# The row factor of a graph attention reaches all partitions through HBM instead of through TensorE

## The reference

```
h = maximum(layernorm(x), 0)
x = x + graph_attention(h, adj, W0, a0)     # layer 0
x = x + multi_relation(h, adj, a0..a3)      # layer 1: scores between nodes, softmax
x = x + relational_conv(h, adj, W, bias)    # layer 2
x = x + elu(graph_attention(h, adj, W3, a3))# layer 3

graph_attention: Wh = h @ W; s1 = Wh @ a1; s2 = Wh @ a2
  e = leaky_relu(s1[i] + s2[j], 0.2); where adj <= 0: -9e15
  out = softmax(e) @ Wh
```

## Time and profile before

| | |
|---|---|
| median of 3 runs | 299.83 us (299.61 to 300.18) |
| profiled execution | 299.55 us, of it the span 297.7 us |
| PE busy | 279.9 us, 94% of the span |
| weight loads of PE (PEld) | 259.4 us, 87% |
| DVE busy | 261.3 us, 88% |
| ACT busy | 260.2 us, 87% |
| POOL busy | 224.8 us, 76% |
| chain that ended last | PE 67%, DVE 20%, ACT 6% |

### The profile page before, as it was taken

The page is one execution under the profiler, slowest core; times in us unless marked ns, Lnnn a source line. Parts: engine busy times, 40 slices in busy tenths (PEclk is TensorE's granted clock), DMA queues, the critical chain, the costliest instruction groups (busy, mean ns, idle before and its releaser), DMA issues.

```text
span 297.7 us, 8186 instructions
## 1 busy us (share of the span) xinstructions
PE 279.9 (94%) x2250; PEld 259.4 (87%) x2250; DVE 261.3 (88%) x1355; ACT 260.2 (87%) x849; POOL 224.8 (76%) x363
## 2 busy tenths in 40 slices
PE   1899999999998999999999999999999899999992
PEld 1799998888987999998888999998888799999991
DVE  2689999888888898999999999988888889799995
ACT  3799997799999985899999889799999998589993
POOL 4987777676776999987768787777677699997800
PEclk9999999999999999999999999999999999999997
DMA  6925555310000000011111660000000000001223
GB/s 185 356 72 160 166 166 148 116 47 0 2 1 2 0 3 1 3 36 55 53 57 53 191 204 1 3 1 2 0 3 0 3 1 0 2 3 36 74 72 107
DMA packets 15949, 17.77 MB, mean 60 GB/s; under 512 B 2720, under 2 KB 11808, under 8 KB 15904
## 3 DMA queue, kind: packets, MB, share of 16 engines
q1 hardware_dynamic: 15072, 17.11, 18.2%
q10 hardware_dynamic: 832, 0.13, 0.3%
HBM read 13.05 MB, written 4.19 MB: 58 GB/s over the span
## 4 chain that ended last, share of the span: by engine, by line
PE 67%; DVE 20%; ACT 6%; issue 3%; DMA 1%; ACTq 0%; DVEq 0%
PE bank L929 19%; PE bank L875 9%; PE bank L880 9%; DVE pT L644 6%; PE bank L851 6%; PE bank L823 5%; PE bank L914 5%; PE bank L900 4%; DVE result L687 4%; DVE st L574 3%; PE bank L926 3%; PE bank L888 2%; PE bank L882 2%; PE bank L838 2%; DVE expy L678 2%
## 5 line engine op out<-in xcount | busy, mean ns | idle before, releaser
L346 POOL TENSOR_TENSOR rs<-ve,minus_half 128x2 f32<-128x2 f32 x128 | 89.9, 702 | 53.7 <-DVE ve L588 51.9
L929 PE MATMUL bank<-val,pT 128*128 128x129 f32 x512 | 74.7, 275 | 0.0
L929 PEld LDWEIGHTS bank<-val,pT 128*128 128x128 f32 x512 | 67.9, 193 | 0.0
L360 POOL TENSOR_TENSOR h<-h,rs 128x256 f32<-128x256 f32 x96 | 59.8, 623 | 0.1
L644 DVE SCALAR_TENSOR_TENSOR pT<-bank,val,edgesT 128x256 f32<-128x256 f32 x128 | 55.8, 478 | 3.7 <-PE bank L888 3.4
L574 DVE BATCH_NORM_STATS2 st<-x 128x6 f32<-128x128 f32 x192 | 44.3, 272 | 0.0
L851 PE MATMUL bank<-w_gat,hT 128*128 128x131 f32 x256 | 42.2, 288 | 0.3 <-ACT hT L447 0.2
L354 POOL TENSOR_TENSOR h<-x,mv 128x256 f32<-128x256 f32 x64 | 39.9, 623 | 2.5
L479 ACT ACTIVATE val<-bank,val 128x128 f32<-128x128 f32 x128 | 41.3, 391 | 0.0
L926 PE MATMUL bank<-ident,vsum 128*128 128x128 f32 x128 | 35.5, 278 | 3.3 <-DVE x L670 1.0
L823 PE MATMUL bank<-ident,h 128*128 128x128 f32 x192 | 38.5, 283 | 0.0
(11 more groups left out here) (80 smaller groups left out, 664.8 us busy)
## 6 DMA issues: line engine op xcount, KB each, us to landing
edges<-in_adj SPq DMA_DIRECT2D x32, 256.0 KB, 3.5
xin<-in_x SPq DMA_DIRECT2D x32, 128.0 KB, 2.7
out_x<-result SPq DMA_DIRECT2D x32, 128.0 KB, 1.7
w_rel<-in_L_gnn_weight SPq DMA_DIRECT2D x1, 256.0 KB, 3.5
w_gat<-in_L_gnn_W ACTq DMA_DIRECT2D x2, 64.0 KB, 3.4
a_rel<-in_L_gnn_a SPq DMA_DIRECT2D x4, 0.5 KB, 4.3
bias<-in_L_gnn_bias SPq DMA_DIRECT2D x1, 64.0 KB, 3.6
a_gat<-in_L_gnn_a ACTq DMA_DIRECT2D x2, 1.0 KB, 3.5
```

Source lines behind the costliest of these rows:

```text
L346: pool.tensor_tensor(rs[:, g % WIDE], ve[:, g % WIDE], minus_half[:, :], ALU.pow).then_inc(rs_ready, 1)
L360: pool.tensor_tensor(h[:, n % HS, :, 0:D], h[:, n % HS, :, 0:D], rs[:, g % WIDE, :].rearrange("p (t o) -> p t o", o=1).to_broadcast([P, T, ...
L929: last = pe.matmul(bank_o(n)[:, t], pT[:, n % 4, u, t * P:(t + 1) * P], values[:, u], start=(u == 0 and layer == 1), stop=(u == T - 1), sk ...
```

## The change

1. The row factor no longer passes PE. `keep_e` (SP) writes the 128 x 2 numbers of a unit from SBUF to one of 8 places of 1 KB in HBM (rows_of_e); `spread_e` (SP) reads such a place 128 times, once for each partition, into e_rows (128 x 256). `take_rows` then waits for e_spread and reads e_rows in SBUF where it read a PSUM bank.
2. All stage lists have another order and other lags. On SP: keep_e lag 5, spread_e 6, loads 10, store 11.
3. `add_eps` is gone: the statistics have three more numbers per node, preset so that the aggregate's variance contains eps; POOL takes the power of that.
4. The weights of layer 3 are loaded by SP between the prefetches, and prepared between units 4 and 7, instead of ahead of all.

```diff
+E_LAG = 5
-SP_LAG = 8
+SP_LAG = 10
@@ SP
+                if k == 2:
+                    sp.dma_start(w_gat[1][:, 0:D], w3).then_inc(gat_loaded[1], 16)
+                    sp.dma_start(a_gat[1][:, :], a3.rearrange("(c p) o -> p (c o)", c=2), allow_slow_non_contiguous=True).then_inc(gat_loaded[1], 16)
...
+            def keep_e(n, layer, g):
+                i, m = nth(GATS, n) % ER, nth(GATS, n)
+                sp.wait_ge(exps_ready, m)
+                if m > ER:
+                    sp.wait_ge(e_spread[i], 16 * ((m - 1) // ER))
+                sp.dma_start(rows_of_e[i].rearrange("t p -> p t"), val[:, g % SLOTS, :, D + 1], allow_slow_non_contiguous=True).then_inc(e_kept[i], 16)
+
+            def spread_e(n, layer, g):
+                i, m = nth(GATS, n) % ER, nth(GATS, n)
+                sp.wait_ge(e_kept[i], 16 * ((m - 1) // ER) + 16)
+                if m > ER:
+                    sp.wait_ge(rows_taken, m - ER)
+                sp.dma_start(e_rows[:, i].rearrange("p t q -> p (t q)"),
+                             rows_of_e[i].rearrange("(o t) p -> o (t p)", o=1).to_broadcast([P, T * P])).then_inc(e_spread[i], 16)
-            pipeline([(load_x, SP_LAG, FIRST), (load_edges, SP_LAG, FIRST), (store, SP_LAG + 1, LAST)])
+            pipeline([(keep_e, E_LAG, FIRST), (keep_e, E_LAG, LAST), (spread_e, E_LAG + 1, FIRST),
+                      (spread_e, E_LAG + 1, LAST), (load_x, SP_LAG, FIRST), (load_edges, SP_LAG, FIRST), (store, SP_LAG + 1, LAST)])
@@ POOL
+            pool.memset(st[:, :, :, 6:8], 0.0).then_inc(ident_ready, 1)
+            pool.memset(st[:, :, :, 8:9], D * EPS).then_inc(ident_ready, 1)
...
-                pool.tensor_tensor(rs[:, g % WIDE], ve[:, g % WIDE], minus_half[:, :], ALU.pow).then_inc(rs_ready, 1)
+                pool.tensor_tensor(rs[:, g % WIDE], mv[:, g % WIDE, :, 1], minus_half[:, :], ALU.pow).then_inc(rs_ready, 1)
@@ DVE
-                dve.wait_ge(rows_put, nth(GATS, n))
+                dve.wait_ge(e_spread[nth(GATS, n) % ER], 16 * ((nth(GATS, n) - 1) // ER) + 16)
...
-                    last = dve.scalar_tensor_tensor(pT[:, n % 4, u], bank_z(n)[:, 0], val[:, k, u, D + 2:D + 3],
+                    last = dve.scalar_tensor_tensor(pT[:, n % 4, u], e_rows[:, nth(GATS, n) % ER].rearrange("p t q -> p (t q)"), val[:, k, u, D + 2:D + 3],
                                                     edgesT[:, g % WIDE, u], ALU.max, ALU.mult)
...
-            pipeline([(mean_and_variance, 2, LAST), (statistics, 1, LAST), (add_x, 14, LAST),
...
+            pipeline([(statistics, 0, LAST), (mean_and_variance, 1, LAST), (invert_sums, 10, LAST),
...
@@ PE
-                else:
-                    pe.wait_ge(exps_ready, nth(GATS, n))
-                    for u in range(T):
-                        last = pe.transpose(z[:, 0, u * P:(u + 1) * P],
-                                            val[:, k, u, D + 1:D + 2].to_broadcast([P, P]), ident[:, :])
-                    last.then_inc(rows_put, 1)
...
-            pipeline([(put_o, 7, LAST), (put_o, 7, FIRST), (put_o, 7, MULTI_REL), (put_z, 5, FIRST),
...
+            pipeline([(put_edgesT, 3, FIRST), (put_z, 3, MULTI_REL), (put_pT, 5, MULTI_REL),
...
```

More of the change, by code:

```diff
@@ L26 @@
 SLOTS = 8
+ER = 8
 HS = 12
@@ L37 @@
 COUNTS = {layers: list(itertools.accumulate(int(layer in layers) for layer, _ in ORDER))
-          for layers in (ALL, ATTEND, GATS, MULTI_REL, RGCN_REL, NOT_LAST, FIRST, LAST)}
-LAG_MAX = 14
-SP_LAG = 8
+          for layers in (NORMED, ALL, ATTEND, GATS, MULTI_REL, RGCN_REL, NOT_LAST, FIRST, LAST)}
+LAG_MAX = 13
+SP_LAG = 10
+E_LAG = 5
 def nth(layers, n):
@@ L64 @@
 TWO_BEFORE = dict(zip(ATTENDING[2:], ATTENDING))
+SCORED = [n for n, (layer, _) in enumerate(ORDER) if layer in NORMED]
+SCORED_BEFORE = dict(zip(SCORED[2:], SCORED))
 def pipeline(stages):
@@ L231, in gat_stack @@
         v_ready = sem("v_ready")
+        e_kept = [sem(f"e_kept{i}") for i in range(ER)]
+        e_spread = [sem(f"e_spread{i}") for i in range(ER)]
         vsum_ready = sem("vsum_ready")
@@ L234, in gat_stack @@
         gathered = sem("gathered")
-        rows_put = sem("rows_put")
         r_ready = sem("r_ready")
@@ L443, in take_hT @@
                 act.wait_ge(hT_put, nth(ATTEND, n))
+                if ORDER[n] == (0, 4):
+                    scale_a(1)
+                    take_wT(1, bank[HT_BANK[n]])
+                if ORDER[n] == (0, 6):
+                    take_wa(1, bank[HT_BANK[n]])
+                if ORDER[n] == (0, 7):
+                    act.wait_ge(norms_put, 1)
+                    act.activation(norm_sums[:, :], bank[HT_BANK[n]][0:1, 500:504], ACT.Copy).then_inc(norms_taken, 1)
                 if layer == 1:
```

136 lines of the change are left out of this document (71 added, 65 removed).

## The result

The changed kernel takes 665.3 us (median of 4 runs, 663.5 to 665.8) where the kernel before takes 299.8: 2.2175 times as long (95% interval 2.2144 to 2.2207). The forecast was 341 in a range of 320 to 357: the direction was right, the size was not. The profiled execution has a span of 664.0 us, 366.3 more than before.

What follows compares the result with a forecast made beforehand. PE was taken to bound the first two layers, DVE's chain of work the last. 299.55 + 18.0 + 20.0 (ring) + 4 (start) + 0 - 1 (end) = 340.6, given as 341 us; range 320 to 357.

Steps and rivals of the forecast that it cites:

- The ring (part 1): Layer 3, 21 steps: result, store, next keep_e, spread, pT, next result; 4.05 us per unit, +18.0 and +20.0.
- fixed terms: Per layer 3 step: result 0.41, to store 0.02, store's issue 0.37, keep_e's issue 0.50, two pT 0.65.
- spread_e issues and lands, 2.1: Layer 3 step: spread's issue to landing, taken from x loads of the same 128 KB; 2.1 us, ends 1.7 and 2.9.
- Rival 1: Spread lands later than a quiet x load, behind keep_e and store; at 2.9, 17 us more, 358; chance 0.11.
- the landing of keep_e: Row factor's write to HBM, issue to landing: 2.3 us at the first unit; elsewhere only its issue, 0.50, was charged.
- The start: First layer 0: keep_e issued after the prefetches, first pT 6.8 us late, partly regained by PE; +4, between 0 and +7.
- Part 3, pT beside GpSimd: Layers 0 and 3: pT with both operands in SBUF and GpSimd block each other; second layer 0 forecast 0, within 3.5.
- a forecast 2.97: Layer 3 step if the ring isn't closed: 2.1 plus two hits of 0.43; a rival totalling 319, chance 0.07.
- hits of 0.43: Layer 3, pT and result: a GpSimd operation gets in between two DVE operations and the second loses 0.43 us.
- Part 4: Eps in the statistics, new orders, late weights: 0 in layers 1 to 3, within 1.5 for order; -1 at the end.

Runs made afterwards that it cites:

- c3_before_sbuf: The kernel before with one operand changed: pT reads its row factor from a tile of ones in SBUF instead of PSUM; 318.8 us (1.065).
- d1: The kernel before with DVE's stage list alone changed: layer 0's statistics, mean_and_variance and add_eps moved to either side of add_x; 302.75 us (1.011).
- d2: The kernel before with eps within the statistics and GpSimd's power held by a semaphore counted up where add_eps stood; 303.1 us (1.011).
- m2_layouts: Transfers alone on SP's queue, no layers computed, row-factor pieces written at several distances in HBM; 9.3 us side by side, 1.60 at 64 bytes.
- c4_before_eps: The kernel before with only eps put into the statistics, 128 DVE instructions less, and GpSimd's power waiting for the variance directly; 302.9 us (1.010).

## Why the prediction was wrong

**The ring (part 1): mechanism right, one term mis-sized.** The order of the queues makes the ring in the units named, 53 to 64 and 117 to 127. Its fixed terms, forecast 0.41 + 0.02 + 0.37 + 0.50 + 0.65, are 0.44 + 0.43 + 0.48 + 0.79. The term "spread_e issues and lands, 2.1" is 7.46. It has two parts. The spread by itself is 3.0 (2.9 in the run of transfers, 3.08 in the kernel without the write), not the 2.1 of an x load: 128 partitions read the same 1 KB, and the x load was not its nearest relative. And 4.4 come of the keep_e issued 0.48 us ahead of it in the same queue: the spread lands 0.2 us behind that keep_e, and in the one step without a keep_e ahead of it, from unit 126 to 127, it lands in 3.3. Rival 1 named that place and priced it at 0.8, by loads beside loads; the write of 4-byte pieces has no relative in the trace of before, and its upper end should have been left far open. The range wasn't even as wide as the prediction's own bounds: it ends at 353, and 2.9 for the spread gives 358. The formula that it quotes from the Trainium skill makes 2.3 of the spread, for 2.9 measured; the section gives it for transfers that GpSimd issues, and these are SP's.

**The step that failed: the landing of keep_e.** The prediction took it as 2.3 at the start, like an x load, and nowhere else. In the ring it charged keep_e's issue alone, 0.50, and in layer 0 it called everything after the start 0. The landing is 7.3 to 14.9, median 9.6. In layer 0 each unit's spread waits for its keep_e, and the keep_e of two units later stands behind that spread in SP's queue, so no more than two are under way; the loads of x and edges go through the same queue (edges 9.1 us, and 3.7 in the kernel without the write). A unit takes 6.9 instead of 2.4: +67.2 and +67.7, where the forecast had 0. In the chain between 27.7 and 131 us the write has 44%, the edge loads 33%, the spread 8%. The start is the same term: the first keep_e issued at 14.11 (forecast 14.3), its spread at 22.27 (forecast 16.6), the first pT at 27.67 (forecast 18.9).

```profile
14.11 0.94 SPq L324 DMA_DIRECT2D rows_of_e<-val  x2
22.27 0.33 SPq L331 DMA_DIRECT2D e_rows<-rows_of_e  x1
```

The runs price it: 268 us between the write side by side and the same write 64 bytes apart (665 to 397), 23 us for that write as such (to 374). The forecast for the kernel without the write is 341 less 21 issues of 0.5, some 330. What was left, 374, is 44 above it, and 21 x (3.08 - 2.1) = 21 of these are the longer spread in the ring; 12 more stand in the second layer 0, which takes 47.7 us for 35.9.

**Part 3, pT beside GpSimd: the mechanism right, its number partly luck.** Five steps without the ring took 2.95 against a forecast 2.97. But the forecast was 2.1 with hits of 0.43 on pT and on result, and here two hits of 0.36 fall on the two pT, on top of 2.2 of other work. By itself, in the old order, it costs 19 us (318.8); the 21 steps have only 6.9 of it (31.1 and 22.8 us instead of 26.6 and 20.5), and the two layers 0 have 9.6, where the forecast for the second was 0 within 3.5. The Trainium skill ("SBUF — State Buffer", two separate sides) has a DVE operation with two SBUF inputs and a GpSimd operation that reads SBUF exclude each other, the first for its whole instruction. The traces agree that it is such inputs that are hit, never pT from PSUM. The size of a hit is smaller than the records of GpSimd's instructions suggest: a pair of hits took 1.58 - 0.87 = 0.71, so 0.36 each, while the GpSimd operation over the first pT had 0.55 of its record left when pT began (152.73 + 0.68 - 152.86). One small term was wrong: pT from SBUF was to take 0.07 less. In c3_before_sbuf it took the same, 467 ns at least.

**Part 4: wrong in sign.** eps was to be worth nothing or a little; alone it costs 3 us. The new orders and late weights without transfers were to be about +3 with the start, and cost 12. That this is DVE's phase against GpSimd was argued, and is shown only in part: in d1 the four steps of 2.63 lost 0.33 each, about one hit, but d2 did not bring the phase back, and what the steps gained was lost in layer 0 and at the start. What in the orders costs the remaining 9 us stays open. So does the sum of the parts: without write and ring the change costs 19, as much as pT's operand alone in the old order, although the orders cost 12 with PE's transposes; the two overlap in a way that no run separates. By the profile of that run the 19 are +6.9 at the start, +10.3 in the layers 0, +6.9 in the 21 steps, +5.4 from unit 48 to 53 and from 112 to 117, and -10.2 from the pT of the last unit of each layer 0 to the first of layer 3, where the forecast had 0 within 1.5; what shortens these isn't shown.

## What to carry to other kernels

A transfer is priced by what it writes and where, not by its bytes: a column of 4-byte numbers written side by side to HBM took 9.3 us, 1.6 at 64 bytes distance. Where a DMA waits for a DMA, both landings stand in the sum, and so does the landing of what stands ahead of it in its queue. For a form of transfer that the trace doesn't show the price is measured first. In a kernel tuned to where two engines meet, an instruction less can cost time: look at what it kept apart.

## What the runs showed of the hardware

- Small writes to HBM close to each other hold each other up. With 16 pieces of 4 bytes per 64 bytes a write of 256 took 9.3 us, with 8 pieces 3.9, 4 pieces 1.87, one 1.60; half as many pieces at the closest distance took 8.4. Four such writes to different places, issued together, took 9.45, as much as one. Reading such a column back takes 2.0 and writing it into SBUF 1.9. The Trainium skill ("DMA: Bandwidth & Descriptors", the table at its start) says that below 512 bytes a DMA does read-modify-write. It names no distance between the pieces; these are all below 512 bytes, and here the distance decides.
- A transfer behind such a write in the same queue lands late too: 13.0 us for the pair, against 7.8 from two queues. In the changed kernel a spread landed 0.2 us behind such a write, 7.4 after its issue, and 3.3 after its issue where none was ahead of it.
- The spread of one 1 KB row to 128 partitions takes 2.9 us, an x load of the same 128 KB 2.06 ((130.91 - 122.67) / 4 in m2_layouts); four spreads issued together 4.9.
- A DVE operation on two SBUF operands that meets one of GpSimd's wide operations grows from 0.40 to 0.75 (expy in c4_before_eps), and two pT in a row from 0.87 to 1.58.
